# Routed expert results: one gather per token and choice after all tiles, against three sweeps over choices sorted by tile, in one ring with x

## Chip, cores and metric

One core of one Trainium2 chip runs the whole program. The metric is the device time of one execution in microseconds (us), taken as the median of several runs.

## The reference, cut to what matters

A batch of 4 x 512 tokens of width 256 goes through a causal attention block and then through a layer with a second attention, a shared feed-forward part and 31 routed experts. Only the last step is touched by the change:

```python
logits = an @ router_w + router_b
aff = softmax(logits); topv, topi = top_k(aff, 3)          # 3 experts per token
gates = sum(one_hot(topi, 31) * topv[..., None], axis=-2)
h = gelu(einsum('bsd,edh->besh', an, re_w1) + re_b1, exact)
routed = einsum('bse,besh,ehd->bsd', gates, h, re_w2) + einsum('bse,ed->bsd', gates, re_b2)
return shared + routed + an + attn_out
```

The kernel computes `h` only for the chosen experts. There are 2048 x 3 = 6144 choices. The choices of one expert fill whole tiles of 128 rows, one expert behind the other, and a choice's position is its row in that order, so a position divided by 128 is the number of the tile that computes it. The program always runs 78 tiles (NT), of which the inputs of the reference fill 62.

With each token's three positions in rising order, the same inputs give these bounds (the number of expert tiles that must be stored before 128 tokens can fetch this choice): for the lowest position 55, 46, 47, 53, 44, 52, 52, 50, 36, 27, 45, 44, 50, 56, 51 and 57 over the 16 token tiles; for the middle one 58, 60, 58 and 61 over groups of four token tiles; for the highest one 62 everywhere. They are worked out from the reference's routing, not read from a profile. The code puts a floor of 48 under each.

## The kernel before, in words

The program runs stage after stage; `mix` (output projection, shared part, router, positions) ends in the lists that `experts` needs, and `experts` is the last stage. Tile sizes are 128 tokens or choices (P) by 256 (D); TILES is 16, TOPK 3, NT 78.

- `mix`, L1797 to L1828, works out `pos`, splits it into `row` and `tile_no`, and turns this round into `c.ids`, the token of each position. `c.experts` holds the expert of each of the 78 tiles and, in its last element, the number of tiles in use.
- `experts` has one loop over tiles on each engine. POOL gathers 128 rows of `an` for tile n into a ring of 12 (L1874, waiting for `turned`, so always 12 tiles ahead of PE). PE turns them (L1913), multiplies by w1 (L1922), ACT applies gelu (L1958), PE multiplies by w2 (L1933), ACT copies the result out of PSUM (L1965) and SP stores it to `ye` in DRAM (L1897). SP marks tile n - 2 as stored, by an increment of `ye_done`, behind its store of tile n (L1899, L1900). DVE copies w1 (L2008) and x (L2010) in each round, with small leftovers of `mix` in rounds 1 to 12 (`close_mix`, `gate_part`).
- After its 78 gathers of x, POOL loads the count of tiles in use into a register (L1877), waits until that many are stored, and issues 48 gathers from `ye` (L1886), three for each token tile, one per choice. They land in a ring of 10 token tiles (30 blocks of 128x256); the last four places of the ring are those of x.
- After its 78 rounds DVE goes token tile by token tile: three additions of gate times result (L2021), each waiting for the one before, and then the bias of the experts, which PE multiplies into one of two PSUM banks (L1948), in a fourth addition (L2025). PE may multiply the bias of tile i only when tile i - 2 is closed. SP stores each finished tile to `out` (L1903).
- `ye` is laid out as "(p n) d": the 128 rows of one tile lie 78 rows apart, and the index is row x 78 + tile (L1999). In `attention2`, L546, SP fills the rows of `ye` that may stay unused.

Orders that matter: POOL has one queue, in which all x gathers stand ahead of all result gathers; DVE's additions stand behind its 78 rounds.

Of the kernel before, what the change touches and what calls it, by code (L numbers as in the profile page):

```python
# [17 lines left out]
P = 128  # L18
# [415 lines left out]
def attention1(nc, c, t):  # L434
# [7 lines left out]
    with a.stack:  # L442
# [34 lines left out]
        def _(sp):  # L477
# [57 lines left out]
            for n in range(2, QUADS):  # L535
# [832 lines left out]
def mix(nc, c, t):  # L1368
# [5 lines left out]
    with a.stack:  # L1374
# [26 lines left out]
        pos, part = a.sb("pos", [P, TOPK, TILES]), a.sb("part", [P, TOPK, TILES])  # L1401
# [296 lines left out]
        def _(dve):  # L1698
# [107 lines left out]
            then(dve.tensor_scalar(c.tile_no[:, :, :], part[:, :, :], ROUNDER, ROUNDER, ALU.add, ALU.subtract))  # L1806
            tick.add(dve.tensor_copy(tile_h[:, :, :], c.tile_no[:, :, :]))
            then(dve.scalar_tensor_tensor(out=c.row[:, :, :], in0=c.tile_no[:, :, :], scalar=-float(P), in1=pos[:, :, :],
                                          op0=ALU.mult, op1=ALU.add))
            row_k = tick.add(dve.tensor_copy(row_h[:, :, :], c.row[:, :, :]))  # L1810
# [22 lines left out]
def experts(nc, c, t, out):  # L1833
# [3 lines left out]
    with a.stack:  # L1837
        MC = FF // P
        XR, YR, RING = 12, 4, 10
        FREE = RING - XR // TOPK  # L1840
        ADDS = TOPK + 1
        y = a.sb("y", [P, RING, TOPK, D])
        xg = y[:, FREE:RING, :, :].rearrange("p i k d -> p (i k) d")
        picked = y[:, 0:2, :, :].rearrange("p i k d -> p (i k d)")[:, 0:TOPK * TILES * E].rearrange("p (k i e) -> p k i e", k=TOPK, i=TILES)
# [5 lines left out]
        tot, inv, slotf = a.sb("tot", [P, TILES]), a.sb("inv", [P, TILES]), a.sb("slotf", [P, TOPK, TILES])  # L1850
        tb, hb, yb, bb = ([a.ps(f"{n}{i}") for i in range(2)] for n in ("tb", "hb", "yb", "bb"))
        gathered = [a.sem(f"gathered{i}") for i in range(XR)]
        stored = [a.sem(f"stored{i}") for i in range(YR)]
        fetched = [a.sem(f"fetched{i}") for i in range(RING)]
        turned, x_copied, w_copied, h_mul, h_done, y_mul, y_copied, ye_done = (a.sem(n) for n in (
            "turned", "x_copied", "w_copied", "h_mul", "h_done", "y_mul", "y_copied", "ye_done"))
        closing = a.sem("closing")
        summed, out_s, b2_in, picked_k, gate_ready, g_turned, g_copied, b_mul = (a.sem(n) for n in (
            "summed", "out", "b2_in", "picked", "gate_ready", "g_turned", "g_copied", "b_mul"))
        block = a.stack.enter_context(nc.Block())  # L1860
        ye = t["ye"].rearrange("(p n) d -> n p d", n=NT)
# [7 lines left out]

        @block.gpsimd  # L1870
        def _(pool):
            for n in range(NT):
                ge(pool, turned, n - XR + 1)
                pool.indirect_dma_start(out=xg[:, n % XR, :], out_offset=None, in_=t["an"],  # L1874
                                        in_offset=bass.IndirectOffsetOnAxis(ap=c.ids[:, n:n + 1], axis=0)).then_inc(gathered[n % XR], 16)

            tiles = pool.value_load(c.experts[0:1, P - 1:P], min_val=TOK * TOPK // P, max_val=NT)  # L1877
            pool.wait_ge(ye_done, tiles)
            pool.wait_ge(gate_ready, 1)
            pool.nop(nofuse=True)  # L1880
            for i in range(TILES):
                if i == FREE:
                    pool.wait_ge(turned, NT)
                ge(pool, summed, ADDS * (i - RING + 1))
                for k in range(TOPK):
                    pool.indirect_dma_start(out=y[:, i % RING, k, :], out_offset=None, in_=t["ye"],  # L1886
                                            in_offset=bass.IndirectOffsetOnAxis(ap=c.slots[:, k, i:i + 1], axis=0))\
                        .then_inc(fetched[i % RING], 16)

        @block.sync  # L1890
        def _(sp):
# [9 lines left out]
            for i in range(TILES):  # L1901
                sp.wait_ge(summed, ADDS * (i + 1))
# [4 lines left out]
        def _(pe):  # L1907
            for r in range(NT + 2):
                if tile(r):
                    pe.wait_ge(gathered[r % XR], 16 * (r // XR + 1))  # L1910
# [228 lines left out]
```

## Time and profile before

| | us |
|---|---|
| runs shown | 1036.88, 1044.26, 1048.63 |
| median of them | 1044.26 |
| profiled execution, its own time | 1046.54 |
| span of the profiled execution | 1044.8 |
| mean granted TensorE clock | 0.939 of full |

All times in the rows below are us from the start of this span, on the one core. A row of a timeline gives start, duration, engine, line, operation, tile written <- tiles read, count, and in brackets the idle time of the engine just before and what released it. PE is TensorE, PEld its weight load, DVE VectorE, ACT ScalarE, POOL GpSimd, SP SyncE; a q behind a name is that engine's sequencer or queue.

### The profile page before, as it was taken

The numbers are of one execution on the slowest core, as the hardware profiler recorded it, in microseconds if no ns is written. First come the engines' busy times: TensorE is split into PE (matmuls) and PEld (weight loads), VectorE is DVE, ScalarE is ACT, GpSimd is POOL, SyncE is SP. The second block draws the span as 40 slices with busy tenths as digits, with TensorE's granted clock in tenths as the row PEclk, the third lists the DMA queues.
The fourth block names the chain that finished last, engine by engine and source line by source line (L and its number), as shares of the span: only waits on it lengthen the run. The fifth ranks groups of instructions, "written<-read, shape, count | busy, mean of one in ns | idle before, by whom it ended". The sixth has DMA issues, their size and how long they took to land. (4 is left out here: it accounts for less than half of the span.)

```text
span 1044.8 us, 18950 instructions
## 1 busy us (share of the span) xinstructions
PE 928.3 (89%) x5522; PEld 691.4 (66%) x5522; DVE 662.1 (63%) x1961; ACT 547.9 (52%) x1371; POOL 480.2 (46%) x614
## 2 busy tenths in 40 slices
PE   7979998997989899659999999897997879999973
PEld 4655555654757576457777776666885669999941
DVE  5866675682796889558777777661455644333365
ACT  5648886784342434347777777751222235555520
POOL 6013663543887878811132333252410066444675
PEclk9989999998999999969999999999999779999975
DMA  7658657434668758889777787626797045445754
GB/s 240 216 165 244 194 181 181 150 108 129 244 225 294 261 212 297 296 226 247 187 199 200 203 218 208 189 90 166 230 299 230 20 117 153 133 136 126 159 161 131
DMA packets 148023, 200.21 MB, mean 192 GB/s; under 512 B 21371, under 2 KB 89754, under 8 KB 147923
## 3 DMA queue, kind: packets, MB, share of 16 engines
q1 hardware_dynamic: 136162, 175.36, 55.0%
q0 software_dynamic: 6048, 16.52, 6.9%
q10 hardware_dynamic: 5712, 7.13, 2.4%
q8 instruction: 47, 0.77, 0.3%
q14 instruction: 54, 0.43, 0.2%
HBM read 121.37 MB, written 77.46 MB: 190 GB/s over the span
## 5 line engine op out<-in xcount | busy, mean ns | idle before, releaser
L990 DVE CUSTOM_DVE_ANT_0 a_sm<-a_sc,keep_mask_qk 128x512 f32<-128x512 f32 (+3 forms) x256 | 118.3, 483 | 64.3 <-PE a_sc L906 62.2
L721 DVE CUSTOM_DVE_ANT_0 rope_x<-a_sc,keep_mask_qk 128x512 bf16<-128x512 f32 (+3 forms) x256 | 112.1, 487 | 55.6 <-PE a_sc L616 50.7
L978 ACT ACTIVATE a_probs<-a_sm,a_neg 128x512 f32<-128x512 f32 (+3 forms) x256 | 140.1, 552 | 8.6 <-DVE a_neg L990 8.6
L1874 POOL DMA_INDIRECT ex_y<-an,keep_ids x78 | 75.3, 965 | 125.1 <-POOLq L61 65.3
L905 PE MATMUL a_sc<-a_ka,a_qa 128*128 128x512 f32 (+3 forms) x256 | 96.3, 377 | 27.2 <-POOL a_ka L887 19.4
L887 POOL CAST a_ka<-a_ka 64x512 fp32r<-64x512 f32 x64 | 38.9, 608 | 176.5 <-DMA a_qa<-qs 175.4
L1281 POOL TENSOR_TENSOR rope_rot<-rope_wqkv 128x512 f32<-128x512 f32 x64 | 94.2, 1490 | 32.9 <-DVE rope_wqkv L1346 32.9
L911 PE MATMUL a_tp<-keep_ident,a_probs 128*128 128x128 f32 x640 | 104.5, 280 | 0.0
L911 PEld LDWEIGHTS a_tp<-keep_ident,a_probs 128*128 128x128 f32 x640 | 74.6, 141 | 25.6 <-issue 17.4
L2008 DVE COPY ex_w<-keep_w 128x514 f32 x78 | 33.5, 430 | 90.7 <-ACT ex_hid L1958 88.2
L1231 PE MATMUL p_ub<-rope_km,rope_wh 128*128 128x512 f32 x256 | 82.0, 402 | 6.0 <-DVE rope_km L1336 6.0
L1922 PE MATMUL ex_hb<-ex_xT,ex_w 128*128 128x128 f32 x624 | 84.1, 279 | 0.0
L918 PE MATMUL a_ob<-a_pt,a_vals 128*64 128x384 f32 (+3 forms) x512 | 82.8, 445 | 0.8 <-ACT a_pt L971 0.8
L1958 ACT ACTIVATE ex_hid<-ex_hb,ex_w 128x128 f32<-128x128 f32 x156 | 48.9, 364 | 63.5 <-PE ex_hb L1922 63.5
L997 DVE COPY a_pt<-a_tp 128x512 f32<-128x512 f32 (+1 forms) x128 | 78.9, 618 | 4.1 <-PE a_tp L911 4.1
L1933 PE MATMUL ex_yb<-keep_o_w,ex_hid 128*128 x312 | 81.0, 383 | 0.0
L906 PE MATMUL a_sc<-a_km,a_qa 128*128 128x512 f32 (+3 forms) x256 | 78.3, 332 | 0.0
L620 PE MATMUL a_st<-rope_qm,rope_km 128*128 128x512 f32 (+3 forms) x256 | 71.6, 354 | 6.9 <-ACT rope_qm L700 2.3
L1922 PEld LDWEIGHTS ex_hb<-ex_xT,ex_w 128*128 128x128 f32 x624 | 77.6, 195 | 0.1
L616 PE MATMUL a_sc<-rope_km,rope_qm 128*128 128x512 f32 (+3 forms) x256 | 66.9, 343 | 10.1 <-PEq L61 5.3
L566 POOL TENSOR_SCALAR_AFFINE_SELECT a_probs<-a_probs 128x128 f32<-128x128 f32 (+1 forms) x120 | 40.2, 338 | 66.7 <-ACT a_probs L689 66.1
L905 PEld LDWEIGHTS a_sc<-a_ka,a_qa 128*128 128x128 f32 x256 | 50.2, 196 | 29.7 <-issue 15.9
(278 smaller groups left out, 2086.1 us busy)
## 6 DMA issues: line engine op xcount, KB each, us to landing
a_qa<-qs SPq DMA_DIRECT2D x128, 128.0 KB, 3.7
ks<-rope_rot SPq DMA_DIRECT2D x40, 256.0 KB, 3.2
qs<-rope_rot SPq DMA_DIRECT2D x40, 256.0 KB, 2.1
ye<-ex_ysb SPq DMA_DIRECT2D x78, 128.0 KB
rope_qm<-qs SPq DMA_DIRECT2D x64, 128.0 KB
rope_km<-ks SPq DMA_DIRECT2D x64, 128.0 KB
qs<-rope_qm SPq DMA_DIRECT2D x32, 256.0 KB, 2.5
vs<-rope_vout SPq DMA_DIRECT2D x16, 512.0 KB, 3.3
```

The source lines that it names most:

```text
L721: return dve.tensor_tensor_reduce(out=junk[:, JUNK[qb]:JUNK[qb] + n], in0=src, in1=c.mask_qk[:, S - n:S], scale=1.0, scalar=-3e38, op0=ALU ...
L905: pe.matmul(out[:, 0:n], qa[:, sl, P * qb:n], ka[:, sl, 0:n], start=True, stop=False)
L906: return pe.matmul(out[:, 0:n], qa[:, sl, P * qb:n], km[:, sl, 0:n], start=False, stop=True)
L911: mm = pe.transpose(tp[:, col:col + P], probs[:, h % PR, JUNK[qb] + P * kb:JUNK[qb] + P * kb + P], c.ident[:, :])
L918: mm = pe.matmul(ob[p % 2][D2 * hh:D2 * hh + D2, P * kb:S], vals[:, p // 2 % VR, kb, h % 4, :], pt[:, h % PT, TCOL[kb]:TCOL[kb] + KLEN[kb] ...
L978: act.activation(probs[:, h % PR, rows(qb)], sm[:, h % SM, rows(qb)], ACT.Exp, bias=neg[:, h % 2, qb:qb + 1], scale=-1.0, accum_out=sums[: ...
L990: return dve.tensor_tensor_reduce(out=sm[:, h % SM, rows(qb)], in0=src[:, 0:n], in1=c.mask_qk[:, S - n:S], scale=-1.0, scalar=3e38, op0=AL ...
L997: dve.tensor_copy(pt[:, u % PT, cols], tp[:, cols]).then_inc(t_dve, 1)
L1231: mm = pe.matmul(bank[:, :], wt[:, k, cols], xt[:, k, b % 2, :], start=(n == 0), stop=(n == 5))
L1281: pool.tensor_tensor(rot[:, u % ROT, half, :], prod[:, u % 2, 2 * half, :], prod[:, u % 2, 2 * half + 1, :], op)\
L1922: mm = pe.matmul(hb[n % 2][:, P * m:P * m + P], w1[:, n % 2, FF * k + P * m:FF * k + P * m + P], xT[:, n % 2, k, :], start=(k == 0), stop= ...
L1933: mm = pe.matmul(yb[n % 2][:, 0:D], hid[:, n % 2, m, :], c.w2[:, bass.ds(e, 1), m, :], start=(m == 0), stop=(m == MC - 1))
```

## The change

What it does, in the order of the data:

1. The three positions of a token are sorted on DVE (min and max), so that choice 0 is the one computed first and choice 2 the one computed last. The gates are brought into the same order by comparison with the unsorted positions. PE turns the sorted positions, DVE takes their maxima, and from these come 16 + 4 integer bounds in SBUF (`bound_i`).
2. `ye` is laid out as "(n p) d", and a position is directly the index of the row.
3. POOL's result gathers go in three sweeps over the 16 token tiles, one per choice. Ahead of each gather of the first sweep, of every fourth of the second and of the first of the third, POOL loads a bound and waits for that many stored tiles (21 waits in place of 1).
4. x and results share one ring of 30 blocks. Gathers of x run 12 tiles ahead at first, 21 at the end.
5. DVE adds in the same three sweeps, each addition waiting for the one before. The bias lies in all eight PSUM banks, two token tiles in each, and is added in pairs (128x512) from the fifth token tile of the last sweep on.
6. SP stores token tile i once its third addition and its bias are done, so all stores of `out` fall into the last sweep.

```diff
-                        rest = t["ye"].rearrange("(p n) d -> p n d", n=NT)[:, least:least + some, :]
+                        rest = t["ye"].rearrange("(n p) d -> p n d", n=NT)[:, least:least + some, :]
...
             for n in range(NT):
-                ge(pool, turned, n - XR + 1)
-                pool.indirect_dma_start(out=xg[:, n % XR, :], ...
+                ge(pool, turned, n + 1 - ahead(n))        # ahead(n) = 12 + 10 * n // NT
+                pool.indirect_dma_start(out=slot(n), ...
-            tiles = pool.value_load(c.experts[0:1, P - 1:P], min_val=TOK * TOPK // P, max_val=NT)
-            pool.wait_ge(ye_done, tiles)
-            pool.wait_ge(gate_ready, 1)
-            pool.nop(nofuse=True)
-            for i in range(TILES):
-                if i == FREE:
-                    pool.wait_ge(turned, NT)
-                ge(pool, summed, ADDS * (i - RING + 1))
-                for k in range(TOPK):
-                    pool.indirect_dma_start(out=y[:, i % RING, k, :], out_offset=None, in_=t["ye"], ...
+            pool.wait_ge(slots_ready, 1)
+            pool.wait_ge(bounds_ready, 1)
+            for k in range(TOPK):
+                for i in range(TILES):
+                    q = NT + TILES * k + i
+                    slot_free(q)          # block q - 30: turned for x, summed for results
+                    if k == 0:
+                        tiles = pool.value_load(bound_i[0:1, i:i + 1], min_val=FEWEST, max_val=NT)
+                    elif k == 1 and i % GROUP == 0:
+                        tiles = pool.value_load(bound_i[0:1, TILES + i // GROUP:TILES + i // GROUP + 1], ...)
+                    elif k == 2 and i == 0:
+                        tiles = pool.value_load(c.experts[0:1, P - 1:P], min_val=FEWEST, max_val=NT)
+                    if k == 0 or k == 1 and i % GROUP == 0 or k == 2 and i == 0:
+                        pool.wait_ge(ye_done, tiles)
+                        pool.nop(nofuse=True)
+                    pool.indirect_dma_start(out=slot(q), out_offset=None, in_=t["ye"], ...
...
             for i in range(TILES):
-                sp.wait_ge(summed, ADDS * (i + 1))
+                sp.wait_ge(summed, TILES * (TOPK - 1) + i + 1)
+                sp.wait_ge(biased, i // 2 + 1)
                 sp.dma_start(out[...], c.base[:, i, :]).then_inc(out_s, 16)
...
+                if r == KEYS_AT:          # PE, round 16
+                    pe.wait_ge(keyed, 1)
+                    pe.transpose(bb[0][0:TOPK * TILES, 0:P], key[...], c.ident[:, :]).then_inc(keys_turned, 1)
+                if r == BOUNDS_AT:        # PE, round 32
+                    pe.wait_ge(keys_reduced, 1)
+                    pe.matmul(bb[1][0:1, 0:TOPK * TILES], top_key[:, :], c.ident[...], ...).then_inc(bounds_mul, 1)
...
             for i in range(TILES):
-                pe.wait_ge(g_copied, i // SB + 1)
-                ge(pe, summed, ADDS * (i - 1))
-                pe.matmul(bb[i % 2][:, 0:D], gateT[:, P * i:P * i + P], b2[:, :], ...).then_inc(b_mul, 1)
+                pe.wait_ge(g_copied, B if i // 2 >= 6 else i // SB + 1)
+                pe.matmul(bias_bank(i // 2)[:, D * (i % 2):D * (i % 2) + D], gateT[...], b2[:, :], ...).then_inc(b_mul, 1)
...
-            for i in range(TILES):
-                dve.wait_ge(fetched[i % RING], 16 * TOPK * (i // RING + 1))
-                for k in range(TOPK):
-                    ge(dve, summed, ADDS * i + k)
-                    dve.scalar_tensor_tensor(out=c.base[:, i, :], in0=y[:, i % RING, k, :], ...).then_inc(summed, 1)
-                dve.wait_ge(b_mul, i + 1)
-                dve.wait_ge(summed, ADDS * i + TOPK)
-                dve.tensor_add(c.base[:, i, :], c.base[:, i, :], bb[i % 2][:, 0:D]).then_inc(summed, 1)
+            for k in range(TOPK):
+                for i in range(TILES):
+                    n = TILES * k + i
+                    q = NT + n
+                    dve.wait_ge(arrived[q % RING], 16 * (q // RING + 1))
+                    ge(dve, summed, n)
+                    dve.scalar_tensor_tensor(out=c.base[:, i, :], in0=slot(q), scalar=weight[:, k, i:i + 1], ...).then_inc(summed, 1)
+                    j = i - BIAS_FROM
+                    if k == TOPK - 1 and 0 <= j < TILES // 2:
+                        dve.wait_ge(b_mul, 2 * j + 2)
+                        dve.wait_ge(summed, TILES * k + min(2 * j + 2, i + 1))
+                        pair = c.base[:, 2 * j:2 * j + 2, :].rearrange("p i d -> p (i d)")
+                        dve.tensor_add(pair, pair, bias_bank(j)[:, :]).then_inc(biased, 1)
+                        if 2 * j + 2 > i + 1:
+                            dve.wait_ge(biased, j + 1)
```

Left out here: DVE's `aside(r)`, which stands in round r + 1 of the 78 and holds the old leftovers in rounds 1 to 13 (with the sorting in rounds 3 to 5 and the integer `slots` in round 6), the weights in rounds 14 to 17, the maxima of the turned positions in round 25 and the bounds in rounds 39 to 42, at most three small instructions in a round; and in `mix` the change of where `pos`, `row` and `tile_no` are kept.

## Rows read from the trace of the kernel before

**Rows 1.** Chain that ended last, the page's part 4.

```profile
PE 15%; DVE 2%; POOL 1%; DMA 1%; issue 1%; POOLq 0%; ACT 0%; DVEq 0%
PE ex_hb L1922 7%; PE ex_yb L1933 7%; PE ex_tb L1913 2%; DVE keep_base L2021 1%; POOL ex_y L1886 1%; DMA ex_y<-ye,keep_slots 1%; DVE keep_base L2025 0%; DMA ex_y<-an,keep_ids 0%; PE ex_tb L1942 0%; POOLq L1837 0%; POOL ex_y L1874 0%; PE ex_bb L1948 0%; ACT keep_ow L1968 0%; DVEq L2024 0%; DVEq L1865 0%
```

**Rows 2.** The end by stretches; busy us and (instructions) of each engine.

```profile
844.00:998.00 154.00, 154.00 (x1076) 142.33 (x1076) 64.96 (x168) 77.15 (x230) 88.23 (x91) 0.98 0.55 142
...
1004.00:1028.00 24.00, 12.67 (x23) 5.42 (x24) 20.63 (x45) 0.00 (x0) 18.21 (x20) 0.55 0.56 162
1028.00:1045.00 17.00, 3.42 (x6) 1.31 (x6) 7.51 (x16) 0.00 (x0) 7.36 (x8) 0.50 0.36 108
```

**Rows 3.** Timeline of POOL, 968 to 977: last x gathers, first result gathers.

```profile
972.67 0.94 POOL L1874 DMA_INDIRECT ex_y<-an,keep_ids  x1 [1.04 <-PE ex_tb L1913]
975.76 0.94 POOL L1886 DMA_INDIRECT ex_y<-ye,keep_slots  x1 [2.15 <-SPq L1900]
```

**Rows 4.** L1877 and L1880, POOL's sequencer, 972 to 977.

```profile
L1877 POOLq TENSOR_LOAD <-keep_experts x1: 496/496/496, 972.4 to 972.4; - x1
L1877 POOLq FUSED_REGOPS  x1: 186/186/186, 973.0 to 973.0; - x1
L1877 POOLq SEQ_ASSERT  x1: 28/28/28, 973.2 to 973.2; - x1
...
L1880 POOLq EVENT_SEMAPHORE  x1: 43/43/43, 975.0 to 975.0; - x1
```

**Rows 5.** L1900, SP's marks of a stored tile, 973 to 976.

```profile
L1900 SPq EVENT_SEMAPHORE  x2: 17/17/17, 973.0 to 975.0; - x2
```

**Rows 6.** Timeline, 996 to 1007: POOL, first additions, bias.

```profile
996.52 1.52 DVE L2021 SCALAR_TENSOR_TENSOR keep_base<-ex_y,keep_gates,keep_base 128x256 f32<-128x256 f32 x3
...
998.12 0.95 POOL L1886 DMA_INDIRECT ex_y<-ye,keep_slots  x1 [0.30 <-issue]
...
1003.58 0.42 DVE L2025 TENSOR_TENSOR keep_base<-keep_base,ex_bb 128x256 f32<-128x256 f32 x1 [5.54 <-PE ex_bb L1948]
...
1005.75 0.42 DVE L2025 TENSOR_TENSOR keep_base<-keep_base,ex_bb 128x256 f32<-128x256 f32 x1
1006.27 1.52 DVE L2021 SCALAR_TENSOR_TENSOR keep_base<-ex_y,keep_gates,keep_base 128x256 f32<-128x256 f32 x3
```

**Rows 7.** Timeline, 1036 to 1041: the last gather and additions.

```profile
1036.55 0.95 POOL L1886 DMA_INDIRECT ex_y<-ye,keep_slots  x1 [0.30 <-issue]
...
1039.35 1.53 DVE L2021 SCALAR_TENSOR_TENSOR keep_base<-ex_y,keep_gates,keep_base 128x256 f32<-128x256 f32 x3 [1.75 <-DMA ex_y<-ye,keep_slots]
1040.98 0.42 DVE L2025 TENSOR_TENSOR keep_base<-keep_base,ex_bb 128x256 f32<-128x256 f32 x1
```

**Rows 8.** L1886 and L1903: from issue to landing, 0 to 1045.

```profile
L1886 POOL DMA_INDIRECT ex_y<-ye,keep_slots x48: 942/946/1126, 975.8 to 1036.5; - x48
...
DMA to landing us min/median/max: 2.7/3.0/3.5
...
L1903 SPq DMA_DIRECT2D out<-keep_base x16: 332/332/338, 1004.1 to 1041.4; - x16
...
DMA to landing us min/median/max: 1.7/2.0/3.6
```

**Rows 9.** Groups by line and shape, 838 to 1045.

```profile
L2008 DVE COPY ex_w<-keep_w 128x514 f32 x78 | 33.5, 430 | 90.7 <-ACT ex_hid L1958 88.2 <-issue 2.6
...
L2021 DVE SCALAR_TENSOR_TENSOR keep_base<-ex_y,keep_gates,keep_base 128x256 f32<-128x256 f32 x48 | 23.3, 485 | 7.8 <-DMA ex_y<-ye,keep_slots 5.5
...
L1942 PE MATMUL ex_tb<-keep_ident,keep_logits 128*31 128x128 f32 x16 | 2.1, 276 | 0.2 <-ACT keep_ow L1968 0.2
...
L1989 DVE TENSOR_TENSOR keep_base<-keep_base,keep_mask_qk 128x512 f32<-128x512 f32 x1 | 0.7, 681 | 0.0
...
L2002 DVE CAST keep_slots<-ex_slotf 128x48 int32<-128x48 f32 x1 | 0.2, 178 | 0.0
```

**Rows 10.** Adds with a PSUM operand, before 840, groups by shape.

```profile
L1741 DVE TENSOR_TENSOR keep_base<-keep_base,mx_yp 128x512 f32<-128x512 f32 x6 | 3.8, 682 | 0.0
```

More of the change, by code:

```diff
@@ L1400, in mix @@
         token_h, row_h, tile_h = (a.sb(n, [P, x, TILES], F16) for n, x in (("token_h", 1), ("row_h", TOPK), ("tile_h", TOPK)))
-        pos, part = a.sb("pos", [P, TOPK, TILES]), a.sb("part", [P, TOPK, TILES])
+        pos, part = c.pos, a.sb("part", [P, TOPK, TILES])
+        row, tile_no = (a.sb(n, [P, TOPK, TILES]) for n in ("row", "tile_no"))
         ow_h = c.ow[:, :, :].rearrange("p k n -> p (k n)").bitcast(F16)
@@ L1805, in _ @@
             then(dve.tensor_scalar(part[:, :, :], pos[:, :, :], 1.0 / P, (P - 1) / (2.0 * P), ALU.mult, ALU.subtract))
-            then(dve.tensor_scalar(c.tile_no[:, :, :], part[:, :, :], ROUNDER, ROUNDER, ALU.add, ALU.subtract))
-            tick.add(dve.tensor_copy(tile_h[:, :, :], c.tile_no[:, :, :]))
-            then(dve.scalar_tensor_tensor(out=c.row[:, :, :], in0=c.tile_no[:, :, :], scalar=-float(P), in1=pos[:, :, :],
+            then(dve.tensor_scalar(tile_no[:, :, :], part[:, :, :], ROUNDER, ROUNDER, ALU.add, ALU.subtract))
+            tick.add(dve.tensor_copy(tile_h[:, :, :], tile_no[:, :, :]))
+            then(dve.scalar_tensor_tensor(out=row[:, :, :], in0=tile_no[:, :, :], scalar=-float(P), in1=pos[:, :, :],
                                           op0=ALU.mult, op1=ALU.add))
-            row_k = tick.add(dve.tensor_copy(row_h[:, :, :], c.row[:, :, :]))
+            row_k = tick.add(dve.tensor_copy(row_h[:, :, :], row[:, :, :]))
             dve.wait_ge(spread, 1)
@@ L1838, in experts @@
         MC = FF // P
[L1839 to L1844, printed above, removed]
+        RING, YR = 30, 4
+        GROUP, FEWEST = 4, TOK * TOPK // P
+        ring = a.sb("ring", [P, RING, D])
         w1 = a.sb("w1", [P, 2, DC * FF + MC])
@@ L1868, in tile, with slot, bias_bank @@
             return 0 <= n < NT
+        def slot(q):
+            return ring[:, q % RING, :]
+        def bias_bank(j):
+            return (bb + hb + yb + tb)[j]
         @block.gpsimd
         def _(pool):
[L1872 to L1875 removed]
@@ new lines, in slot_free @@
+            def slot_free(q):
+                last = q - RING
+                if 0 <= last < NT:
+                    pool.wait_ge(turned, last + 1)
+                elif last >= NT:
+                    pool.wait_ge(summed, last - NT + 1)
+            for n in range(NT):
+                ge(pool, turned, n + 1 - ahead(n))
+                pool.indirect_dma_start(out=slot(n), out_offset=None, in_=t["an"],
+                                        in_offset=bass.IndirectOffsetOnAxis(ap=c.ids[:, n:n + 1], axis=0)).then_inc(arrived[n % RING], 16)
@@ L1984, in close_mix, with over_places, gate_of, aside @@
-            def close_mix(r):
-                dve.wait_ge(closing, r)
+            tick = Tally(tick_s)
+            def over_places(x):
+                return x.rearrange("p (o i) -> p o i", o=1).to_broadcast([P, TOPK, TILES])
+            p0, p1, p2 = (c.pos[:, k, :] for k in range(TOPK))
+            def gate_of(k):
+                return c.gates[:, :, k:k + 1].rearrange("p i o -> p o i").to_broadcast([P, TOPK, TILES])
+            def aside(r):
                 if r < 2:
                     half = c.base[:, TILES - SB + 2 * r:TILES - SB + 2 * r + 2, :].rearrange("p i d -> p (i d)")
-                    dve.tensor_add(half, half, c.last[r]).then_inc(closing, 1)
+                    tick.add(dve.tensor_add(half, half, c.last[r]))
```

118 lines of the change are left out of this document (79 added, 39 removed).

## The prediction

> **What bounds the kernel now.** I read the page's chain first, then the stage table, then the timeline of the last 75 us, then the sequencer instructions of the lines that the change moves. In the chain [rows 1] the reader sees PE for most of it and, behind PE, DVE additions, POOL gathers and their DMA. The stretches [rows 2] put these in order. From 844 to 998 PE is busy all of the time; this is the loop over 78 tiles, and its period is what POOL shows beside it: 1.04 idle + 0.94 busy = 1.98 us a tile [rows 3]. From 1004 to 1028 DVE is busy 20.6 of 24 us, and PE has little to do. After 1028 neither is busy half of the time. So the loop is bound by PE and the 41 us behind it by how results come and are added; only the latter can be changed by this diff.
>
> Two chains run in that end. POOL's: the first result gather starts at 975.76, right behind SP's mark at 975.0 [rows 3, 5], and the 48th at 1036.55 [rows 7]: 60.8 us for 47 steps. The one at 998.12 [rows 6] is the 18th, so a step takes 22.36/17 = 1.315 us beside the loop and 38.43/30 = 1.281 us after it. DVE's: it adds three times at 996.52 and then waits 5.54 us for the first bias [rows 6]; from there a token tile takes 1.63 + 0.52 = 2.15 us (1.52 of additions and 0.11 of wait, 0.42 of bias and 0.10 of wait) [rows 6]. At the end DVE waits for the last gathers (1.75 us idle), which landed 39.35 - 36.55 = 2.8 us after they started, and ends at 1041.40 [rows 7]. Both chains have to shrink, or the other one holds the end.
>
> **POOL's chain after the change.** The mark at 975.0 is the 62nd: the two marks of rows 5 stand at 973.0 and 975.0, and counting back from the end of the loop in steps of 1.98 us gives 62 for the second, as the routing does. The first bound is 55, seven tiles earlier: 975.0 - 7 x 1.98 = 961.1, and with the same 0.76 us from mark to gather the first result gather starts at 961.9, 13.9 us earlier. The later bounds of the first sweep (at most 57) and of the second (58 to 61) are met long before POOL arrives there. The last x gather is no obstacle: it now waits for tile 57 instead of 66 and starts at about 972.67 - 9 x 1.98 = 954.9. Nor is the ring: gather 13 of the results needs tile 62 turned, at 964.8, and comes at about 979.
>
> With before's steps, 27 beside the loop and 20 after it, the 48th gather starts at 961.9 + 27 x 1.315 + 20 x 1.281 = 1023.0.
>
> Then the 20 added waits. What queues behind each is every later gather, and DVE waits for those. Loading a register took POOL's sequencer 0.50 + 0.19 + 0.03 us, 0.8 us from 972.4 to 973.2 with the gaps, and the wait's nop 0.04 [rows 4]. But it began at 972.4, before the gather in front of it started on POOL (972.67 [rows 3]): the sequencer runs ahead, and the load lies beside the gather's 0.94 us. From nop to gather took 0.7 us, so that the gather at 972.67 was sent at about 972.0, and the sequencer was held some 0.45 us by it. That makes 0.45 + 0.8 + 0.1 = 1.35 us of sequencer for a bounded gather, beside 1.25 us of POOL (0.95 + 0.30 [rows 6]). The lower end is 0 a wait (all hidden). The upper end is 0.8 + 0.1 + 0.7 - 0.3 = 1.3 us, if the sequencer can't be ahead while gathers stand back to back, which no row shows. I take 0.15, near the 1.35, since row 4 shows the overlap itself: 20 x 0.15 = 3.0, and the last gather starts at 1026.0. The Trainium skill (DMA: Bandwidth & Descriptors, Latency and other measured facts) gives a floor of about 600 ns for such a load; the 0.50 here is a little under it. By that figure, unhidden, 20 loads would be an estimated 12 us, which speaks against this change.
>
> It lands 2.8 us later and needs one addition of 0.5: 1029.3.
>
> **DVE's chain.** It starts at 996.5 as before, without the 5.54 us. One addition takes 1.52/3, some 0.51, 0.52 with its wait [rows 6]: 48 x 0.52 = 25.0. A pair's bias is one add of 128x512 with PSUM, 0.68 each [rows 10]; before, 16 of 0.42 + 0.10. The first four pairs wait for nothing recent and overlap their neighbours by some 0.08 (0.60), the last four have 0.10 of wait (0.78): 5.5 us. DVE would end at 1027.0. PE can be no obstacle: its turns end at 1003, and 16 bias products at before's pace of 1.2 us a product would be 19 us, but they no longer wait for DVE, and the first pair is needed only at 996.5 + 36 x 0.52 = 1015. The lower end for this chain is 1026, the upper end POOL's.
>
> So POOL sets the end, by 2.3 us. That is narrow: whatever else POOL gains, DVE gives back.
>
> **The rest.** PE gets one turn (0.28 us for such a product [rows 9]) and one smaller product in its loop: +0.3 us, between 0 and 0.6, on both chains. DVE's asides: the largest in before's loop (0.68 us [rows 9]) stood beside PE, as ACT held DVE back for 1.2 us a round (88.2/78 [rows 9]); three of 0.2 us (0.18 for 128x48 [rows 9]) fit as well: 0. If that cover were gone they would cost 3 us in all. The new layout of `ye` keeps 1 KB runs in both directions; neither its stores nor its gathers are seen with another pitch in this trace, so from the landing times 2.7 to 3.5 us [rows 8] I bound it at -0.3 to +0.7 and take 0. The same for the fill in `attention2`: 0. The 14 added semaphores: 0.
>
> Beside the loop a gather took up to 1.13 us, and 0.94 at best [rows 8]; ten more of them now stand there, and at 1.315 against 1.281 us a step that is 0.3 us, already in the sum. By the Trainium skill (SBUF — State Buffer, SBUF: two separate sides) a f32 copy on DVE locks POOL out while it writes descriptors; were each of the ten held for a whole copy of 0.43 us, it would be an estimated 4 us, which the rows contradict.
>
> The stores of `out` are a real cost. Before, 16 of them were spread over 37 us at 2.0 us each [rows 8]. Now a pair of token tiles comes free every 1.3 us (0.52 + 0.78), 262 KB, or 200 GB/s, beside a gather of 131 KB every 1.28 us, 100 GB/s. Before, 162 GB/s took 0.56 of the DMA engines [rows 2], so full use would be about 290 GB/s: the last sweep runs at that limit. A gather or the last store then lands later by 0 to 1.6 us (3.6 was the slowest store [rows 8], 2.0 the median). I take 0.5.
>
> **The sum**, against the profiled execution: DVE's last instruction moves from 1041.4 to 1029.3 + 0.3 = 1029.6, -11.8; the stores give back 0.5: -11.3. Its own time of 1046.54 becomes 1035.2; from the median of 1044.26, 2.3 lower, the time is 1033.0.
>
> **Rivals.**
> A. The waits serialise on POOL (the other side). Place: POOL's queue, L1880's successor, in the first sweep. At 1.3 us a wait the last gather starts at 1023.0 + 26 = 1049, the end of the additions is 1052.6, 11.2 later than before: 1055. It decides from (1041.4 - 0.3 - 0.5 - 1026.3)/20 = 0.7 us a wait. For it: the gap of 0.30 between gathers never shrank, so how far the sequencer is ahead isn't seen. Against it: rows 4 and 3, the load that began before the gather.
> B. The DMA engines are full in the last sweep. Gathers land at 5 us and the stores queue behind them: +4 us on my sum, 1037. For it: the 290 GB/s above. Against it: the landing was 2.8 us at a share of 0.56, and the overlap lasts only 12 us.
> C. The bounds open nothing (the change doesn't do what it says): the ring or the bound of some token tile holds the first sweep to the 62nd tile. Then POOL's chain is before's plus the waits, and DVE's gain is hidden: 1044. Against it: the routing gives 57 as the largest bound of that sweep.
> D. DVE is the end (waits wholly hidden, stores harmless): 1027.3, which makes 1030. Its gain beyond my forecast is small for the reason above.
>
> **How the numbers follow.** My forecast, with D as its near end, 0.58 (its own range 1029 to 1036); B 0.16; C 0.10; A, or a cost of 0.5 us and more for a wait, 0.16. About 1% is what a measurement can tell here from no change, 10.4 us: below 1033.8 is faster, above 1054.7 slower. The forecast stands at that edge; with its lower half and D I give faster 0.50. Slower needs the upper part of A: 0.10. The rest, 0.40, is within 1%. The runs before lie 12 us apart, which widens the range at both ends: 1026 to 1049.
>
> **What would show it.** In the profile after: the first result gather near 962 (step 1 of POOL's chain); its first 16 gathers in steps of 1.25 to 1.45 us, where 1.9 and more would be A; the 48th near 1026; no wait of DVE for PE's bias, additions in steps of 0.52 from 996.5 on; DVE's last sweep waiting a little for gathers; 16 stores from about 1017 on and a DMA share of 0.8 or more there (B: landing of 4 us and more). PE's loop must keep 1.98 us a tile. I am wrong if the first gather isn't before 965, if bounded gathers stand 1.9 us apart, or if the loop is longer by more than 1 us.

## The result, and the profile after

The changed kernel takes 1033.72 us in the median of 20 runs, the kernel before 1044.63 in as many; the ratio is 0.9887 with a 95% interval of 0.9868 to 0.9906. That is faster by 1.1%, at the edge of what I had called faster (1033.8); the forecast was 1033.0. One of the 20 runs of the changed kernel took 1383.20 us at a mean granted clock of 0.605; it counts in the median and not in the ratio.

The profiled spans are 1029.6 us after and 1044.8 before, 15.2 us apart, and 4.0 of these lie ahead of the last stage: the first gather of x starts at 834.55 after and at 838.55 before, and ahead of it stand stages in which the diff changes next to nothing. Their end varies from run to run (833.96 to 842.11 over the profiles of the table below), so I compare the last stage by times from its first gather of x. The page of the kernel after, its chain:

```profile
PE 15%; DVE 3%; issue 1%; DMA 0%; POOL 0%; DVEq 0%; ACT 0%; POOLq 0%
PE ex_hb L1954 7%; PE ex_yb L1965 6%; DVE keep_base L2099 2%; PE ex_tb L1945 2%; DMA ex_ring<-an,keep_ids 0%; DVE keep_base L2107 0%; POOL ex_ring L1899 0%; DVEq L1870 0%; DVE ex_xT L2088 0%; ACT ex_hid L2000 0%; DVE ex_w L2086 0%; PE ex_bb L1973 0%; DVEq L2105 0%; PE ex_bb L1970 0%; DVEq L2086 0%
```

DVE's additions have gone from 1% to 2% of the span, and POOL's gathers of results and their DMA have left the line, against [rows 1]. The stretches of the end of the kernel after (stretch, its length, busy us and instructions of PE, PEld, DVE, ACT, POOL, then PEclk, DMA share, GB/s):

```profile
992.50:1004.00 11.50, 11.26 (x62) 9.19 (x61) 9.58 (x21) 4.69 (x12) 8.76 (x10) 0.91 0.52 148
1004.00:1012.00 8.00, 6.42 (x16) 4.47 (x14) 6.33 (x13) 0.00 (x0) 6.17 (x7) 0.50 0.39 112
...
1018.00:1030.00 12.00, 0.00 (x0) 0.00 (x0) 7.22 (x13) 0.00 (x0) 2.65 (x3) 0.50 0.62 196
```

The reader sees DVE busy for most of the time up to its last addition, which ends at 1026.14, where in [rows 2] it was idle for half of the last 17 us. The timeline of POOL, after (start, duration, engine, line, operation, tile <- tiles read, count, idle before and releaser):

```profile
951.20 0.95 POOL L1899 DMA_INDIRECT ex_ring<-an,keep_ids  x1 [1.03 <-PE ex_tb L1945]
959.29 0.95 POOL L1917 DMA_INDIRECT ex_ring<-ye,keep_slots  x1 [7.15 <-PE ex_tb L1945]
960.54 0.95 POOL L1917 DMA_INDIRECT ex_ring<-ye,keep_slots  x1 [0.30 <-issue]
961.79 0.95 POOL L1917 DMA_INDIRECT ex_ring<-ye,keep_slots  x1 [0.30 <-issue]
...
970.57 1.10 POOL L1917 DMA_INDIRECT ex_ring<-ye,keep_slots  x1 [0.30 <-issue]
...
994.45 0.95 POOL L1917 DMA_INDIRECT ex_ring<-ye,keep_slots  x1 [0.30 <-issue]
...
1020.32 0.94 POOL L1917 DMA_INDIRECT ex_ring<-ye,keep_slots  x1 [0.30 <-issue]
```

The first result gather comes 124.74 us after the first gather of x, against 137.21 before [rows 3, 5], and the 48th at 185.77 against 198.00 [rows 7]. The steps of the bounded sweep are 1.24 to 1.42 us, 1.28 on average, where before had 1.315 beside the loop, and the gap is still 0.30: a load and a wait ahead of each gather show nowhere. The timeline of DVE, after:

```profile
992.51 0.42 DVE L2088 COPY ex_xT<-ex_tb 128x256 f32<-128x256 f32 x1
992.85 11.11 DVE L2099 SCALAR_TENSOR_TENSOR keep_base<-ex_ring,ex_weight,keep_base 128x256 f32<-128x256 f32 x19
1004.41 10.54 DVE L2099 SCALAR_TENSOR_TENSOR keep_base<-ex_ring,ex_weight,keep_base 128x256 f32<-128x256 f32 x18 [0.46 <-DVE keep_base L2099]
1014.88 0.68 DVE L2107 TENSOR_TENSOR keep_base<-keep_base,ex_bb 128x512 f32<-128x512 f32 x1
...
1016.86 0.68 DVE L2107 TENSOR_TENSOR keep_base<-keep_base,ex_hb 128x512 f32<-128x512 f32 x1
...
1018.04 0.69 DVE L2107 TENSOR_TENSOR keep_base<-keep_base,ex_hb 128x512 f32<-128x512 f32 x1
...
1023.17 0.69 DVE L2107 TENSOR_TENSOR keep_base<-keep_base,ex_tb 128x512 f32<-128x512 f32 x1
1023.89 2.25 DVE L2099 SCALAR_TENSOR_TENSOR keep_base<-ex_ring,ex_weight,keep_base 128x256 f32<-128x256 f32 x4
```

The 5.54 us wait for PE [rows 6] is gone and so are the waits for gathers [rows 7]. But 18 additions take 10.54 us, 0.59 us a step where [rows 6] have 0.51 (1.52 for three). The sequencer shows what stands between them (L1870 is `ge`, the wait on the addition before; x47 is the 48 additions but one):

```profile
L1870 DVEq EVENT_SEMAPHORE  x47: 21/21/50, 993.4 to 1025.6; - x47
...
L2099 DVE SCALAR_TENSOR_TENSOR keep_base<-ex_ring,ex_weight,keep_base x48: 474/483/542, 992.8 to 1025.7; 128x256 f32<-128x256 f32 x48
```

The stores of `out`, after:

```profile
L1935 SPq DMA_DIRECT2D out<-keep_base x16: 332/332/451, 1015.6 to 1026.2; - x16
...
DMA to landing us min/median/max: 1.7/2.9/3.3
```

Their landing has a median of 2.9 us in place of 2.0 [rows 8], but from DVE's last addition to the end of the span it takes 3.46 us, and 3.40 before. The gathers of results land with the same median as in [rows 8]; the slowest takes 4.2 us in place of 3.5:

```profile
L1917 POOL DMA_INDIRECT ex_ring<-ye,keep_slots x48: 942/949/1205, 959.3 to 1020.3; - x48
...
DMA to landing us min/median/max: 2.7/3.0/4.2
```

### The profile page after: what moved, and what is told of

The parts are those of the page before. It is cut to its first block and busy times, and to the rows that moved or that the text cites. A ratio compares the mean times of both kernels' runs of the same rounds, so it can differ in the third digit from the quotient of the medians.

```text
span 1029.6 us, 19079 instructions
## 1 busy us (share of the span) xinstructions
PE 922.3 (90%) x5525; PEld 692.0 (67%) x5525; DVE 663.4 (64%) x1972; ACT 547.7 (53%) x1371; POOL 481.9 (47%) x614
## 5 line engine op out<-in xcount | busy, mean ns | idle before, releaser
L1899 POOL DMA_INDIRECT ex_ring<-an,keep_ids x78 | 75.9, 973 | 106.5 <-POOLq L61 64.8
```

## The experiments

All ran beside the kernel before. In this table all times but the last two columns are us from the first gather of x in the profile of each: the start of the first and of the last result gather, the start of the first addition, and the end of the last one (with the bias, where that comes last).

| kernel | first gather | last gather | first addition | last addition ends | ratio to before | interval |
|---|---|---|---|---|---|---|
| before | 137.21 | 198.00 | 157.97 | 202.85 | 1 | |
| after | 124.74 | 185.77 | 158.30 | 191.59 | 0.9887 | 0.9868 to 0.9906 |
| e0, the changed kernel again | 124.52 | 185.77 | 158.32 | 191.60 | 0.9841 | 0.9802 to 0.9880 |
| e1, waits swapped | 124.23 | 185.88 | 158.16 | 190.30 | 0.9837 | 0.9805 to 0.9869 |
| e2, additions free | 123.10 | 191.26 | 157.15 | 195.66 | 0.9896 | 0.9870 to 0.9922 |
| e3, no bounds | 137.51 | 197.74 | 158.30 | 202.18 | 0.9997 | 0.9969 to 1.0024 |
| e4, pace of 12 | 135.96 | 196.11 | 158.39 | 200.37 | 0.9953 | 0.9918 to 0.9988 |
| e5, loads doubled | 125.61 | 193.88 | 158.57 | 198.04 | (1041.89 us, one run) | |
| e6, before with eight banks | 137.14 | 198.17 | 157.91 | 203.04 | 0.9984 | 0.9950 to 1.0017 |
| e8, marks earlier | 125.07 | 186.65 | 157.22 | 190.91 | 0.9876 | 0.9834 to 0.9918 |
| e11, chained in pairs | 124.38 | 186.31 | 158.37 | 190.59 | 0.9916 | 0.9883 to 0.9949 |

The last stage repeats to 0.2 us between the first two profiles of the changed kernel, which separates what the ratios, with intervals of 0.4 to 0.8%, do not. In the profiles of e2 and e8 the loop itself was shorter by about 1.1 us (first addition at 157.15 and 157.22), though nothing in it was made faster; counted from the first addition, the end comes after 33.3 us in e0, 32.1 in e1, 38.5 in e2, 33.7 in e8 and 32.2 in e11. The runs e7, e9 and e10 are not in the table; why, stands with e10.

**e0: the scale.**

> The changed kernel once more, as the scale for the others. Theory T: DVE's chain of 48 chained additions (steps of 0.59 us) and 8 bias additions sets the end; POOL's gathers are over about 2.3 us before they are needed. Rival R: POOL's gathers and their landing set the end. Both expect about 1034 us, a ratio of 0.989 to the kernel before, and from the first gather of x to DVE's last addition 191.6 us, as in the profile at hand.

Measured: 191.60 us, and a ratio of 0.9841. The stage is that of the profile at hand.

**e3: the early start undone.**

```diff
-                    if k == 0:
-                        tiles = pool.value_load(bound_i[0:1, i:i + 1], ...)
-                    elif k == 1 and i % GROUP == 0:
-                        ...
-                    elif k == 2 and i == 0:
+                    if k == 0 and i == 0:
                         tiles = pool.value_load(c.experts[0:1, P - 1:P], ...)
-                    if k == 0 or k == 1 and i % GROUP == 0 or k == 2 and i == 0:
                         pool.wait_ge(ye_done, tiles)
```

> POOL waits once, for all 62 tiles in use, ahead of the first result gather; the 20 other loads and waits go. Everything else is as changed (ring, sweeps, bias, pacing). The early start alone is undone. Theory: first result gather at 12 to 13 us later, steps of 1.28 us, so the last gather starts about 12.5 us later and POOL sets the end by 10 us: 202 us from the first gather of x to the last addition, 1044 us, as the kernel before. Rival (the gain came from the bias and the sweeps on DVE, the early start is worth little): at most 194 us, 1036 us.

Measured: 202.18 us and a ratio of 0.9997. Ring, sweeps, pacing and the bias in eight banks stay, and with no early start all of the gain is gone but 0.7 us. DVE waits for gathers again, as in [rows 7]:

```profile
1034.22 0.48 DVE L2094 SCALAR_TENSOR_TENSOR keep_base<-ex_ring,ex_weight,keep_base 128x256 f32<-128x256 f32 x1 [0.48 <-DMA ex_ring<-ye,keep_slots]
1035.66 0.48 DVE L2094 SCALAR_TENSOR_TENSOR keep_base<-ex_ring,ex_weight,keep_base 128x256 f32<-128x256 f32 x1 [0.96 <-DMA ex_ring<-ye,keep_slots]
```

**e6: the bias alone.**

```diff
-                ge(pe, summed, ADDS * (i - 1))
-                pe.matmul(bb[i % 2][:, 0:D], gateT...
+                pe.matmul((bb + hb + yb + tb)[i // 2][:, D * (i % 2):D * (i % 2) + D], gateT...
...
-                dve.wait_ge(b_mul, i + 1)
+                dve.wait_ge(b_mul, 2 * (i // 2) + 2)
```

Left out are two waits of PE ahead of the products, for the last uses of the banks in the loop, and the bank's name in DVE's addition.

> The kernel before, with the bias products in all eight PSUM banks, so that none waits for an addition; the bias is still added per token tile. One part of the change alone. Theory (both chains have to shrink): DVE's wait for the first bias falls from 5.5 us to about 6 at most, its catching up gets shorter, but the last gather lands when it did, so the end stays: 202.8 us from the first gather of x to the last addition, 1045 us. Rival (the freed DVE was the gain): 3 us and more off the end.

Measured: 203.04 us and 0.9984, so nothing. DVE's first wait for the bias did not get shorter (5.97 us, 5.54 before): the first bias is added 165.40 us after the first gather of x, 165.03 before, since PE has its turns of the gates to do first:

```profile
1001.47 0.42 DVE L2026 TENSOR_TENSOR keep_base<-keep_base,ex_bb 128x256 f32<-128x256 f32 x1 [5.97 <-PE ex_bb L1949]
...
1037.06 1.53 DVE L2022 SCALAR_TENSOR_TENSOR keep_base<-ex_y,keep_gates,keep_base 128x256 f32<-128x256 f32 x3 [1.75 <-DMA ex_y<-ye,keep_slots]
```

With e3 this shows one side of the "both chains" reading: DVE freed alone gives 0 (e6) to 0.7 us (e3), the early start on top of it 10.6 us. The other side, the early start without the sweeps on DVE, was not tried. An estimate from [rows 6]: with the first bias at 1003.58 and 2.15 us a token tile, DVE's old order ends at 1003.58 + 15 x 2.15 + 0.42 = 1036.25 however early the gathers come, 5.2 us before 1041.40. So some 6 of the 11.3 us would need the new work of DVE.

**e4: the pacing undone.**

```diff
-                return 12 + 10 * n // NT
+                return 12
```

> Gathers of x stay 12 tiles ahead of PE to the end, as in the kernel before, in place of 12 to 21. Theory (the pacing is what lets the result gathers start early, since they stand behind all x gathers on POOL): the last x gather starts at 134.4 us after the first and the first result gather at about 135.7, 11 us later than changed; POOL sets the end: 201 us from the first gather of x to the last addition, about 1043 us. Rival (the pacing changes nothing that ends last): 191.6 us, 1033 us.

Measured: first result gather at 135.96, last addition over at 200.37 (expected 135.7 and 201), ratio 0.9953. Without the pacing 8.8 of the 11.3 us are gone, since the bounds open nothing while x gathers stand in front:

```profile
973.20 0.94 POOL L1899 DMA_INDIRECT ex_ring<-an,keep_ids  x1 [1.03 <-PE ex_tb L1945]
974.62 0.94 POOL L1917 DMA_INDIRECT ex_ring<-ye,keep_slots  x1 [0.48 <-issue]
975.87 0.95 POOL L1917 DMA_INDIRECT ex_ring<-ye,keep_slots  x1 [0.30 <-SPq L1931]
```

The first result gather follows the last x gather within 0.48 us, and no wait for a mark stands between them.

**e5: the price of a bounded gather.**

```diff
                     if k == 0:
                         tiles = pool.value_load(bound_i[0:1, i:i + 1], ...)
+                        pool.wait_ge(ye_done, tiles)
+                        pool.nop(nofuse=True)
+                        tiles = pool.value_load(bound_i[0:1, i:i + 1], ...)
```

> Each of the 16 gathers of the first sweep has its register load, wait and nop twice. Theory (POOL's sequencer runs ahead of POOL, so a load costs nothing until the sequencer itself is the longer; 0.45 us a gather + 0.6 a load + 0.1 by the forecast's reading): steps of the first sweep of 1.75 to 1.9 us in place of 1.28, 7 to 9 us later on POOL, of which 5 to 7 show at the end. If a load costs less of the sequencer than that, the steps stay at 1.28 and nothing changes; if it stood in POOL's way in full, steps would have been above 1.28 in the changed kernel already.

Measured: steps of the first sweep of 1.85 us on average, with gaps around 0.75 us where POOL had 0.30:

```profile
970.05 0.94 POOL L1920 DMA_INDIRECT ex_ring<-ye,keep_slots  x1 [1.06 <-SPq L1934]
971.75 0.94 POOL L1920 DMA_INDIRECT ex_ring<-ye,keep_slots  x1 [0.75 <-SPq L1934]
...
977.07 0.94 POOL L1920 DMA_INDIRECT ex_ring<-ye,keep_slots  x1 [0.73 <-PE ex_tb L1948]
978.76 1.18 POOL L1920 DMA_INDIRECT ex_ring<-ye,keep_slots  x1 [0.75 <-issue]
```

The shortest step is 1.68 us (977.07 to the next, at 978.76, is 1.69); the average holds waits for marks too. The last gather comes 8.1 us later than in the changed kernel and the end 6.4, both within what was expected. So the sequencer runs ahead, one load and wait fit under the 1.25 us of a gather, and a second pair makes the sequencer the longer of the two, by 0.43 us at the least and 0.6 on average. That is the forecast's picture with one load a little cheaper: the loads of `bound_i` took 0.29 + 0.15 us in the kernel after, where [rows 4] had 0.50 + 0.19.

```profile
L1909 POOLq TENSOR_LOAD <-ex_bound_i x16: 285/288/575, 951.1 to 975.1; - x16
L1909 POOLq FUSED_REGOPS  x16: 147/147/181, 951.6 to 975.4; - x16
```

**e1: what makes an addition's step 0.59 us.**

```diff
-                    dve.wait_ge(arrived[q % RING], 16 * (q // RING + 1))
                     ge(dve, summed, n)
+                    dve.wait_ge(arrived[q % RING], 16 * (q // RING + 1))
```

> In DVE's additions the two waits change places: first the one on the addition before, then the one on the gather. Theory T, in the form that the 0.07 us more than forecast for each addition are the wait on the addition before standing as an instruction of its own behind the other: steps of 0.52 in place of 0.59 us, 48 x 0.07 = 3.4 us off DVE's chain, of which some 2 us show before the last gather's landing takes over: 189.5 us from the first gather to the last addition. If the step is 0.59 whatever the order (two waits cost it), nothing changes: 191.6. Rival R: the step may fall, the end does not move: 191.6.

Measured: 37 additions in a row in 19.35 us, 0.52 a step, as forecast. The instruction of the sequencer is still there, but now it is the wait on the gather (L2098). The end comes 1.3 us earlier, at 190.30 (189.5 was expected), and DVE now waits for gathers:

```profile
L2098 DVEq EVENT_SEMAPHORE  x48: 21/21/50, 994.1 to 1026.0; - x48
...
994.40 19.35 DVE L2099 SCALAR_TENSOR_TENSOR keep_base<-ex_ring,ex_weight,keep_base 128x256 f32<-128x256 f32 x37
...
1021.88 0.48 DVE L2099 SCALAR_TENSOR_TENSOR keep_base<-ex_ring,ex_weight,keep_base 128x256 f32<-128x256 f32 x1 [0.54 <-DMA ex_ring<-ye,keep_slots]
...
1026.06 0.48 DVE L2099 SCALAR_TENSOR_TENSOR keep_base<-ex_ring,ex_weight,keep_base 128x256 f32<-128x256 f32 x1 [0.87 <-DMA ex_ring<-ye,keep_slots]
```

The order in the code decides which of the two waits stands as an instruction of its own: it is the one written last, in the changed kernel `ge` on the addition before, in e1 the wait on the gather. Written last should be the wait that is over early, here the gather's. Of 3.4 us on DVE's chain 1.3 show, the rest is POOL's. In the ratio (0.9837 against 0.9841 of e0, measured beside it) this can't be told from nothing.

**e2: additions that don't wait for one another.**

```diff
-                    ge(dve, summed, n)
+                    ge(dve, summed, n - TILES + 1)
```

> Each addition waits only for the addition to the same token tile in the sweep before (16 back), no longer for its neighbour. Theory T: steps of about 0.40 us, DVE catches up with POOL in the second sweep and the end is the last gather's landing plus one addition: 189.3 us from the first gather of x to the last addition, 2.3 less than the changed kernel, about 1031.5 us. Rival R: no change of the end, 191.6, and 1034 us.

Measured: the steps of 0.40 us came, and both ends were wrong. The end is at 195.66, 4.1 us later than e0 (5.2 counted from the first addition). The medians of six runs each, measured side by side, are 1036.69 and 1030.03 us; the ratios, 0.9896 and 0.9841, have intervals that touch (0.9870 to 0.9922 and 0.9802 to 0.9880). DVE, then POOL:

```profile
993.66 11.56 DVE L2099 SCALAR_TENSOR_TENSOR keep_base<-ex_ring,ex_weight,keep_base 128x256 f32<-128x256 f32 x29
1007.91 0.48 DVE L2099 SCALAR_TENSOR_TENSOR keep_base<-ex_ring,ex_weight,keep_base 128x256 f32<-128x256 f32 x1 [2.69 <-DMA ex_ring<-ye,keep_slots]
```

```profile
996.51 1.22 POOL L1917 DMA_INDIRECT ex_ring<-ye,keep_slots  x1 [0.30 <-issue]
998.03 8.01 POOL L1917 DMA_INDIRECT ex_ring<-ye,keep_slots  x1 [0.31 <-issue]
1006.34 0.94 POOL L1917 DMA_INDIRECT ex_ring<-ye,keep_slots  x1 [0.30 <-issue]
```

DVE adds at 0.40 us a step, 29 times without a gap, and one gather on POOL takes 8.01 us, where 0.95 is usual. It ends at 1006.04, 0.8 us after the row of additions at 1005.22. The held gather is the 30th, and the row ends after 29 additions, since the next one needs its result. Meanwhile nothing is moved at all (the stretch 1001 to 1005.2, columns as above):

```profile
1001.00:1005.20 4.20, 4.20 (x21) 3.61 (x20) 4.20 (x11) 0.00 (x0) 4.20 (x1) 0.98 0.00 0
```

DVE then waits 2.69 us for a gather, and the last gather starts 5.5 us later than in e0. Three gathers in the first 4 us of the same row had passed in 0.95 to 1.22 us; why the fourth was held and these not stays open.

**e10 and e9, e11: what keeps POOL out.**

```diff
 e10, on e2
-                    dve.scalar_tensor_tensor(out=c.base[:, i, :], in0=slot(q), scalar=weight[...], in1=c.base[:, i, :], ...)
+                    dve.tensor_reduce(c.base[:, i, k:k + 1], slot(q), AX.X, ALU.add)
 e9 and e11, on the changed kernel
-                    dve.wait_ge(arrived[q % RING], 16 * (q // RING + 1))
-                    ge(dve, summed, n)
+                    ge(dve, summed, n if n % 2 == 0 else n - TILES + 1)
+                    dve.wait_ge(arrived[q % RING], 16 * (q // RING + 1))
```

> As e2 (nobody waits for the neighbour), but each addition is a sum over the block's 256 columns into one column of the base: one SBUF input in place of two. The weighting and adding of results is left out. Theory P in its narrow form (it is the second SBUF input that keeps POOL out): DVE's row is as dense as in e2, yet no gather is longer than 1.3 us and the last one starts at 185.8 us after the first gather of x. Rival Q (a dense row of any DVE instructions keeps POOL out): one gather as long as the rest of the row, 6 to 12 us.

> Every second addition waits for its neighbour, the others only for the sweep before. Between e1 (all wait: POOL's gathers at most 1.2 us) and e2 (none waits: one gather of 8.0 us, over only when DVE's row of 29 additions was). Theory P (a gather on POOL gets through only in a gap between DVE instructions with two SBUF inputs): gaps remain after every second addition, so the longest gather stays below 2 us, additions take some 0.46 us on average, and the end is POOL's, as in e1: 190.3 us from the first gather of x to the last addition. Rival Q (the busy share of DVE is what counts): the longest gather is some 3 to 5 us, the end 192 us or later.

> The kernel of e9 once more, since on the chip of e9 the loop over tiles took longer in both kernels. Theory P: no gather longer than 1.3 us, additions 0.46 us apart on average, DVE waits for POOL's last gathers, and 189.8 to 190.3 us from the first gather of x to the last addition, against 191.6 of the changed kernel and 190.3 of e1. Rival Q (the busy share of DVE counts): gathers of more than 2 us and an end later than 191.6.

e10, DVE and then all gathers of results:

```profile
1026.89 12.16 DVE L2099 TENSOR_REDUCE keep_base<-ex_ring 128x1 f32<-128x256 f32 x37
```

```profile
L1917 POOL DMA_INDIRECT ex_ring<-ye,keep_slots x48: 942/946/962, 977.0 to 1049.6; - x48
```

37 instructions in 12.16 us without a gap, and the longest of the 48 gathers took 0.96 us. So a dense row of DVE instructions alone doesn't keep POOL out. The reductions differ from the additions of e2 in three things: one input from SBUF in place of two, one column written in place of 256, and 0.33 us a step in place of 0.40. The second input is the likeliest of the three, but no run separates them. The forecast for e10's last gather did not come true (212.41 us): on that chip the kernel before took 1088.23 us, and the loop over tiles in e7, e9 and e10 is 30 us longer than elsewhere, so the times of e7, e9 and e10 are of use only for single instructions.

e9 and e11 have a gap after every second addition, 0.46 us a step on average. The longest gathers were 1.19 and 1.17 us; e11's:

```profile
L1917 POOL DMA_INDIRECT ex_ring<-ye,keep_slots x48: 942/975/1166, 963.4 to 1025.3; - x48
```

and the end in e11 was at 190.59, ratio 0.9916 (e9, with four runs: 0.986, 0.9797 to 0.9922). Q fell in all three: DVE was as dense in e10 and nearly so in e9 and e11, and no gather took 2 us. P holds in what it said of the gathers; its end of 189.8 to 190.3 was missed by 0.3 us. It is no rule for each gather, as three in e2 passed, and the stall itself was seen in one trace; that it comes in most executions of e2 is only suggested by its six runs, 1035.45 to 1039.14.

**e8: marks one tile earlier, on e1.**

```diff
-                if n >= 2:
-                    sp.wait_ge(stored[(n - 2) % YR], 16 * ((n - 2) // YR + 1))
+                if n >= 1:
+                    sp.wait_ge(stored[(n - 1) % YR], 16 * ((n - 1) // YR + 1))
```

> The changed kernel with the waits swapped as in e1, and SP marks tile n - 1 as stored behind its store of tile n, not tile n - 2: each mark comes one tile (1.98 us) earlier, if the store has landed by then. Theory (with the waits swapped POOL's gathers set the end): first result gather 1.5 to 2 us earlier, last one too, and from the first gather of x to the last addition 188.8 us against 190.3 in e1, DVE's chain being the floor. Rival (DVE alone sets it): 190.3.

Measured: first result gather at 125.07, later than in e1, and the end at 190.91. SP's waits say why:

```profile
SPq L1931 <- DMA ye<-ex_ysb: 44.5, 40, 3.2
```

40 marks of 78 had to wait for their store to land, up to 3.2 us: one tile earlier, it is the landing of the stores that sets the marks. The marks that POOL waits for first did not come earlier, so the run doesn't decide between its theory and its rival. In the kernel after 10 marks had to wait, and four stand between 953 and 960, at 954.2, 957.9 (3.7 us behind the one before), 958.5 and 959.4:

```profile
SPq L1931 <- DMA ye<-ex_ysb: 9.1, 10, 2.4
...
L1931 SPq EVENT_SEMAPHORE  x4: 17/17/17, 954.2 to 959.4; - x4
...
L1931 SPq EVENT_SEMAPHORE  x1: 17/17/17, 958.5 to 958.5; - x1
```

The mark at 958.5 is the 55th, the first bound (the 62nd stands at 971.3, and seven steps of 1.98 us back would be 957.4), and the first result gather starts 0.8 us behind it, as it did behind its mark in the kernel before. That is why it came 1.1 us late: forecast 123.6 us after the first x gather, measured 124.74. What held the stores there isn't shown.

**e7: the layout of `ye` alone, in the kernel before.**

> The kernel before with ye laid out as (n p), the index being tile x 128 + row; nothing else changes. Theory: the layout is worth nothing, 202.8 us from the first gather of x to the last addition and a ratio of 1.00; landing of result gathers at a median of 3.0 us as before. Rival (the contiguous tile changes stores and gathers): the landing moves by 0.3 us or more, or the ratio leaves 1 by 0.3%.

Measured: a ratio of 1.0009 (0.9957 to 1.0062). No effect was found, but the interval is wider than the 0.3% that the rival asks for. The stage took 247.93 us on that chip, and its profile gives no landing times, so the run itself doesn't decide. The landing of result gathers in the changed kernel, a median of 3.0 us as before, speaks for the theory.

No kernel of these is clearly faster than the changed one: e1 and e11 end 1.0 to 1.3 us earlier in the profile, and their ratios don't show it.

## Why the prediction was right

The time moved by -10.9 us in the medians and by -11.2 in the profile's last stage (191.59 + 3.46 against 202.85 + 3.40); -11.3 was forecast. Behind the total the forecast of each chain was wrong, and that the end came out within 0.5 us is luck. Counted from the first gather of x, POOL's chain was to end at 191.05 and would have ended at 190.2, an estimate (185.77 + 3.9 + 0.5, with the landing of e1); DVE's was to end at 188.75 and ended at 191.59. The forecast named the wrong chain, and the right one came to nearly the same number.

- **What bounds the kernel: right.** The loop kept its length (158.30 to the first addition, 157.97 before: +0.33, forecast +0.3 for two more PE products). All gain is in the end. DVE freed alone gives 0 to 0.7 us (e6, e3); that the early start alone isn't enough either is an estimate.
- **The first gather: right within 1.1 us.** Forecast 123.6, measured 124.74, the rest being a late mark (shown with e8).
- **The cost of a bounded gather: 3.0 us in the sum, measured next to 0.** The 47 steps take 61.03 us, 60.23 without the waits (e3), and the gaps are equal. The reading of [rows 3, 4] that the load lies beside the gather was right (e5); the step that failed is the 1.35 us of sequencer, read from a single load that took 0.50 us. The loads of the kernel after are shorter. Rival A fell with it: the gap stayed 0.30.
- **DVE's chain: forecast 30.5 us, measured 33.3.** The failed step is the 0.52 us an addition, taken from [rows 6], where additions two and three of a token tile have one wait. Each addition of the change has two, and the chained one stood apart: 0.59. e1 brings the 0.52 back.
- **So which chain ends last: wrong.** I had POOL over DVE by 2.3 us; it is DVE that ends last, with POOL's last gather started 5.8 us before DVE is done, of which landing and an addition take 3.3 by the forecast and 4.4 in e1. With 0.59 in place of 0.52, the forecast of DVE's chain would have been 188.75 + 48 x 0.07 = 192.1, within 0.5 us of the measured end.
- **The stores: 0.5 us in the sum, measured 0.06.** They do land later (2.9 against 2.0 us), but the last one doesn't hold the end. What the term leaves out shows where POOL ends last: the last gather's block is added 3.9 us after the gather's start in e1 and 4.0 in e3, where 2.8 was forecast. That is why e1 ended at 190.30 and not at 189.5. In both the stores of `out` fall into the last sweep; that they are what delays the gather isn't shown. The DMA share from 1018 on was 0.62, not 0.8 and more, and the median gather landed in 3.0 us, not 5: rival B fell. That full use would be about 290 GB/s isn't shown by any run; 196 GB/s took a share of 0.62.
- **Rival D had the mechanism, which I gave only as the near end:** DVE is the end, the waits are wholly hidden, the stores harmless. Its time, 1030, was too low by the same 0.07 us an addition. **Rival C** fell with e3 against e0: the bounds do open the gathers.
- **Additions that wait for one another: not priced at all.** I carried the wait from the code into the 0.52 and asked only what it costs. e2 shows what it buys: without it one gather on POOL took 7 us longer. Nothing in the trace before showed such a stall; its additions were chained as well.

## What to carry to other kernels

Where two chains share an end, price each step of both with the waits that the new code gives it, down to how many waits an instruction has and which of them comes last; of two waits, put the one that is over early last. And a wait on one engine may be what lets another work: before taking out waits between DVE additions with two SBUF inputs, look whether POOL has gathers to issue beside them, and look for one that takes many times its usual time. Gathers on one queue are moved forward by what stands ahead of them (the x gathers, 8.8 us) as much as by their own condition.

## What was not expected of the hardware

- A row of 29 DVE additions (128x256 f32, both inputs in SBUF) at 0.40 us a step held one gather on POOL for 8.01 us, to 0.8 us behind the row's end. With every addition, or every second one, waiting for the one before (steps of 0.59 and 0.52 us, or 0.46 on average) the longest gather was 1.2 us, and beside 37 reductions with one input and one column of output 0.96. The Trainium skill (SBUF — State Buffer, Who interferes with whom) says that a DVE instruction with two SBUF inputs contends with a GpSimd instruction that reads SBUF; by that rule, if a gather's index counts as such a read, e2 and e10 agree, but for the three gathers of e2 that passed. The same section says that a probe with `tensor_tensor` was not seen to stall a DMA issued from GpSimd; e2, with a multiply and add of two SBUF inputs, shows one that was held, for a whole row of instructions.
- POOL's sequencer works ahead of POOL: a register load, a wait and a nop per gather cost nothing, and a second set 0.4 to 0.6 us a gather (e5).
- On DVE a second wait costs 0.07 us a step when the late one of the two stands as an instruction of its own, and nothing in the other order (e1).
